# Gated network: where TensorE issues the second column's first-layer products among the third layer's waves

## The reference

```python
h = silu(_tlin(x, w1_w, w1_s)) * _tlin(x, w2_w, w2_s)   # 128 -> 512
h = gelu(_tlin(h, h1_w, h1_s))                           # 512 -> 512
h = gelu(_tlin(h, h2_w, h2_s))                           # 512 -> 512
return _tlin(h, w3_w, w3_s)                              # 512 -> 128
# _tlin(x, w, s) = einsum('bsi,oi->bso', x, w) * s, w has the values -1, 0, 1
```

## Time and profile before

| | us |
|---|---|
| median of three runs | 2126.95 (2126.47 to 2128.80) |
| the profiled execution | 2126.03 |
| its span, first to last instruction | 2124.1 |
| TensorE / VectorE / ScalarE busy | 2019.2 / 1648.8 / 1433.4 |
| mean granted TensorE clock | 0.978 of full speed |

### The profile page before, as it was taken

How to read it: one execution, slowest core, us unless ns; L and a number is a source line. 1 busy time by engine, 2 the same in 40 slices (tenths; PEclk the granted TensorE clock), 3 DMA queues, 4 the chain that set the end, 5 groups by cost and what they waited for, 6 DMA issues and landing times. The chain is left out here.

```text
span 2124.1 us, 40168 instructions
## 1 busy us (share of the span) xinstructions
PE 2019.2 (95%) x14693; PEld 1356.0 (64%) x14693; DVE 1648.8 (78%) x3999; ACT 1433.4 (67%) x1915; POOL 615.6 (29%) x859
## 2 busy tenths in 40 slices
PE   2899999999999999997899999799999996999998
PEld 1577777777777777776444444577777773444443
DVE  3888988888988888873666775577777766999997
ACT  1688777888777888774577776566666663555554
POOL 1344444544444544443000000233333330000000
PEclk9899999999999999997899999899999997999999
DMA  6000000000000000001564553000000000000000
GB/s 167 21 21 20 12 21 21 21 21 21 11 21 21 21 21 21 12 21 31 135 131 106 107 121 81 1 2 2 2 2 2 2 2 1 11 16 11 16 11 20
DMA packets 55361, 69.37 MB, mean 33 GB/s; under 512 B 13008, under 2 KB 32640, under 8 KB 55168
## 3 DMA queue, kind: packets, MB, share of 16 engines
q1 hardware_dynamic: 55168, 66.82, 13.4%
HBM read 45.30 MB, written 4.72 MB: 24 GB/s over the span
## 5 line engine op out<-in xcount | busy, mean ns | idle before, releaser
L864 POOL TENSOR_SCALAR_AFFINE_SELECT pr<-pr 128x512 f32<-128x512 f32 x256 | 202.4, 814 | 371.1 <-ACT pr L795 371.1
L422 PE MATMUL a_pO<-va,pr 128*128 128x66 f32 x2048 | 303.1, 271 | 1.9 <-POOL pr L864 1.5
L422 PEld LDWEIGHTS a_pO<-va,pr 128*128 128x128 f32 x2048 | 272.0, 192 | 18.9 <-issue 15.4
L1614 ACT ACTIVATE c_pr<-c_pS 128x1536 f32<-128x1536 f32 x128 | 186.0, 1453 | 119.2 <-PE c_pS L1426 119.2
L1669 POOL TENSOR_SCALAR_AFFINE_SELECT c_pr<-c_pr 128x512 f32<-128x512 f32 x256 | 158.4, 643 | 264.8 <-DVE c_pr L1534 264.8
L761 ACT ACTIVATE sq<-a_pW 128x512 f32<-128x512 f32 x192 | 114.4, 597 | 148.5 <-PE a_pW L363 145.8
L789 ACT ACTIVATE th<-a_pS 128x1536 f32<-128x1536 f32 x128 | 186.0, 1453 | 30.1 <-PE a_pS L407 29.6
L423 PE MATMUL a_pO<-va,pr 128*128 128x66 f32 x1024 | 198.2, 275 | 0.0
L795 ACT ACTIVATE pr<-th 128x1536 f32<-128x1536 f32 x128 | 190.5, 1489 | 3.1
L407 PE MATMUL a_pS<-qs,k 128*128 128x512 f16 (+1 forms) x1024 | 187.3, 326 | 0.9 <-issue 0.9
L1534 DVE TENSOR_SCALAR c_pr<-c_pr 128x1536 f32<-128x1536 f32 x128 | 122.6, 958 | 78.4 <-ACT c_pr L1614 78.4
(11 more groups left out here) (245 smaller groups left out, 4425.1 us busy)
## 6 DMA issues: line engine op xcount, KB each, us to landing
b_cwB<-b_by_expert SPq DMA_DIRECT2D x64, 512.0 KB, 8.5
k<-k SPq DMA_DIRECT2D x64, 256.0 KB, 3.6
x<-in_L_attn_tokens_dram SPq DMA_DIRECT2D x8, 512.0 KB, 7.1
out_dram<-x SPq DMA_DIRECT2D x16, 256.0 KB, 2.3
d_h<-in_L_ffn_h_w_dram SPq DMA_DIRECT2D x2, 1024.0 KB, 7.7
b_by_expert<-b_cwT SPq DMA_DIRECT2D x64, 8.0 KB, 1.8
wmod<-in_L_wmod_dram SPq DMA_DIRECT2D x2, 384.0 KB, 4.1
d_w<-in_L_ffn_w_w_dram SPq DMA_DIRECT2D x3, 256.0 KB, 3.2
```

Of the source, the lines that this page charges most:

```text
L422: pe.matmul(out, w[:, hh * N + t * P:hh * N + (t + 1) * P], v[:, 0, p, :], start=True, stop=t == 0)
L864: last = gp.affine_select(out=part, in_=part, compare_op=ALU.is_ge, fill=0.0, base=0, pattern=[[0, HPG], [1, P]], channel_multiplier=-1)
L1614: act.activation(pr[g][:, :, :], pS[:, :, 0:N + P], ACT.Exp, scale=float(1.0 / np.sqrt(np.float32(DQ)))).then_inc(s_ex, 1)
```

## The change

The third wave of the third layer is issued in two parts. Its first two blocks (four matmuls) go ahead of pA of column 1, its other three blocks (six matmuls) between pA and pB of column 1. So pB of column 1 comes behind the whole third wave. The waits of the wave stay with its first block. On ScalarE hi of column 0 and tanh of column 1 change places. In the first pass (n = -1) only ScalarE's exchange has an effect, since there is no third layer yet; in the last one (n = 15) the wave's two parts follow each other.

```diff
-        def pe_hidden(pe, n, layer, w):
+        def pe_hidden(pe, n, layer, w, first=0, end=HT * HT):
-            for m, (i, o) in enumerate(wave[w]):
-                if m == 0:
+            for m, (i, o) in enumerate(wave[w][first:end]):
+                if first == m == 0:
...
                 if 0 <= n < RUNS:
                     pe_third(pe, n, 1)
+                if 0 <= n < RUNS:
+                    pe_third(pe, n, 2, 0, 2)
                 if 0 <= n + 1 < RUNS:
                     pe_first(pe, n + 1, 1, 0)
+                if 0 <= n < RUNS:
+                    pe_third(pe, n, 2, 2)
+                if 0 <= n + 1 < RUNS:
                     pe_first(pe, n + 1, 1, 1)
                 if 0 <= n < RUNS:
-                    pe_third(pe, n, 2)
                     pe_third(pe, n, 3)
...
                 if 0 <= n + 1 < RUNS:
+                    act_hi(act, n + 1, 0)
                     act_tanh(act, n + 1, 1)
-                    act_hi(act, n + 1, 0)
```

More of the change, by code:

```diff
@@ L1795, in pe_second, with pe_third @@
             pe_hidden(pe, n, 0, w)
-        def pe_third(pe, n, w):
-            pe_hidden(pe, n, 1, w)
+        def pe_third(pe, n, w, first=0, end=HT * HT):
+            pe_hidden(pe, n, 1, w, first, end)
         def pe_out(pe, n, i):
```

## The result

The changed kernel takes 2135.21 us (median of seven executions), the kernel before 2126.95 (seven): 8.3 us more. The ratio over all of them is 1.0035 with a 95% interval of 1.0024 to 1.0047; it goes with the means (2134.57 and 2127.04), while the medians alone give 1.0039. The kernel is slower, as forecast (2133.5, range 2130.0 to 2137.0), by a little more than forecast. The profiled execution has a span of 2133.8 us, against 2124.1 before.

What follows compares the result with a forecast made beforehand. It took the second wave's deadline on VectorE's low 1, with 0.10 us spare, as what matters; 0.22 + 1.04 + 13 x 0.45 - 0.5 = +6.6 us gave a median of 2133.5 us, range 2130.0 to 2137.0.

Steps and rivals of the forecast that it cites:

- (a): TensorE, column 1: four third-wave matmuls ahead of pA start it at 6.48; its wait for gf goes, -0.26 us.
- (b): TensorE, column 1: six matmuls ahead of pB remove its 0.36 us wait but make uf on VectorE 0.55 us late.
- (c): ScalarE's swap of hi 0 and tanh 1: tanh at 7.18, gf at 7.90, hidden behind pB; zero cost, bound 0.05.
- (d): VectorE from uf 1 to low 1: same uninterrupted list, 4.44 us, so low 1 runs 13.30 to 13.98.
- (e): TensorE before second layer's second wave: new 1.07 us wait for low 1 replaces 0.62; wave starts 0.45 later.
- (f): From second wave to next stretch: unchanged, gapless 6.92 us, nothing catches up; next start 20.95.
- The ends: Outside the steady stretches: start +0.22 us (bounds 0 and 0.6), first stretch +1.04, last stretch -0.5, tail unchanged.
- 1 (nothing replaces the waits): Faster: TensorE's two waits go without a new one before the second wave; -8.8 us, 2118.2; chance 0.06.
- 2 (no change): Second wave's new wait no longer than the old ones; only the ends (+0.8) remain, 2127.7; chance 0.12.
- 4 (the exchange sets the delay): ScalarE's swap, not pB, makes uf 1 0.31 late and the wave 0.21 late: 2130.5; chance 0.05.
- 3 (the clock falls in the new pause): TensorE's clock drops in each run's 1.07 us pause, 17 us more: 2150; chance 0.03.
- The rule weighed ahead of the sum: Weight-load busy time (9.39 of 20.50 us) measures TensorE's headroom; VectorE is contended, closing waits worth nothing; sum uses neither measure.

Runs made afterwards that it cites:

- e1: Changed kernel with ScalarE's order put back as before, leaving TensorE's part alone: ratio 1.0046 against the kernel before, stretches of 21.03 us.
- e3: Kernel before with TensorE's order four third-wave matmuls, pA, pB, other six matmuls; ScalarE as before: ratio 1.001, stretches of 20.64 us.
- e10: Kernel before with pB of column 1 alone moved behind the third layer's third wave: one time, 2140.01 us beside a median of 2128.03.
- run 0: No experiment: a pass of the kernel's last stage, without addition to x; its stretch took 19.91 us before the change, 21.04 after.
- run 14: No experiment: a late pass of the kernel's last stage, without transposes for a following pass; its stretch took 20.37 us before the change, 19.96 after.
- e5: e4 plus two VectorE moves, normalisation to the head of the pass and cast of hx ahead of low 3: 2117.92 us, ratio 0.9961.
- e4: Kernel before with one third-wave block ahead of pA 1, one between pA and pB, three behind: ratio 0.9994, stretches of 20.40 us.
- e7: Kernel before with only e5's two VectorE moves, TensorE and ScalarE as before: ratio 1.0002, stretches of 20.50 us.
- e6: Changed kernel, with ScalarE's exchange, plus e5's two VectorE moves: ratio 0.9976 against the kernel before, stretches of 20.01 us.

## Why the prediction was right, point by point

- **The two waits go, (a) and (b).** Right: pA 1 at 6.47, pB 1 at 8.20.
- **pB's place sets VectorE, (b).** Right as a mechanism (e1, e3, e10), mis-sized by 0.10: I took 0.05 us from a matmul's end to the instruction that it releases, from a tanh on ScalarE. uf starts 0.15 behind pB's end, after the change (2062.05 to 2062.20) as in e10 (2001.69 to 2001.84). I had 0.15 as the outer bound.
- **The exchange hides, (c).** Right in the steady runs: tanh 7.18, gf 7.88, and e1 has the change's stretch.
- **The list behind uf 1, (d), and the new pause, (e).** 4.42 us against 4.44; the pause is 1.16 us against 1.07, larger by the mis-sized release.
- **Nothing catches up, (f).** Right: from the second wave's start to the next stretch 6.93 us against 6.92. Steady price 0.53 a run, inside 0.40 to 0.60 and above the 0.45 taken; over thirteen runs this is 6.92 us against 5.85.
- **The ends.** Run 0 +1.13 (forecast +1.04), run 14 -0.41 (-0.5), the tail unchanged. The start was the weak term: +1.33 in the profiled execution against +0.22. The mechanism counted there is real: from pA 0 to pA 2 the change takes 0.20 us more (5.27 against 5.07). But 0.25 had come ahead of pA 0, where the transposes already ran slower (0.88 us against 0.63), and the other 0.88 came behind pA 2, with the clock at 0.53 in 1794.17 to 1796.17, where it had been 1.00 at the same distance before. Bounds of 0 to 0.6 did not hold it, because the clock was no term of the start.
- **The rivals.** 1 (nothing replaces the waits) needed low 1 by 12.91. e5, where it ends at 12.82 (2010.32 + 0.68 in a stretch from 1998.18), shows that this point decides and what it is worth: 19.87 us. 2 (no change) needed low 1 to end by 13.53; it ended at 14.05. 4 (the exchange sets the delay) fell with uf 1's wait for pB, and with e1. 3 (the clock falls in the new pause) fell: the pause is in every run and the clock is at 1.00 in all fifteen stretches. The clock did cost time, but before run 0.
- **The rule weighed ahead of the sum.** The Trainium skill, Perfetto Trace Analysis, section Identifying the Most-Contended Engine, names two measures for TensorE, the products done against their peak (MFU) and weight-load busy time; the prediction took the second alone. Weight loads were busy for 9.55 of e5's 19.87 us, in which TensorE had no pause left, so here they do not show its headroom. TensorE's waits alone were worth 0.10 us (e4), close to the nothing that the prediction drew from the rule, but VectorE's shorter list alone was worth nothing either (e7).

The sum in the last stage is 1.13 + 6.92 - 0.41 = 7.6 us without the start, 9.0 with it; the ratio's 0.35% is 7.4 us. The span grew by 9.7 us where 6.6 were forecast. The 3.1 between them are 0.74 ahead of the stage, 1.11 in its start, 1.07 in the thirteen stretches and 0.09 in each of the runs 0 and 14: all on one side, so no error hid another.

## What to carry to other kernels

Work moved ahead of a waiting product fills the pause, but whatever that product feeds starts later; follow it through the next engine's list to the next deadline, and ask how much is spare there (here 0.10 us against a delay of 0.63, for a net loss of 0.53). A pause that is closed on one engine is worth its length only if the other engine's chain, from its trigger to the next thing that is waited for, gets shorter too: here each half gave at most 0.10 us a run, both together 0.63. Take work off that chain that has no near deadline (the normalisation of two runs ahead) and put it where the engine idles.

## What the runs showed of the hardware

- A VectorE instruction that waits for a matmul into the bank it reads started 0.15 us behind the matmul's recorded end in the change and in e10, and 0.14 in e6 (2008.58 + 0.60, then 2009.32), while tanh on ScalarE started 0.05 behind. The addition to x started 0.05 behind the last transposes, too (2120.02 + 0.65, then 2120.72, in the kernel before), so it isn't VectorE as such; why uf takes longer is open.
- The same kernel's start took 17.50 or 19.03 us, depending on when TensorE's clock came up from its lower level (granted clock 1.00 or 0.50 from 12 to 14 us behind run 0's transposes), and the time up to the stage differed by up to 5.9 us between kernels with the same code there (run 0's transposes at 1779.44 in e4, at 1785.36 in e1). The steady stretches repeated within 0.02 us. A difference of 0.1% in the whole can't be read from single times, but the stretches show it.
